# Gate values that travel with the rows, gathers that add, and a channel mix whose first norm runs inside the time mix

## The reference, cut to what matters

```python
x = x + delta_memory(layernorm(x))          # three recurrences, 16 chunks of work ("turns")
# mixture of experts: 8 experts, 2 of them per token
probs = softmax(xf @ w_router); topk_w, topk_idx = top_k(probs, 2)
h   = gelu(einsum('td,edh->teh', xf, w1) + b1)
out = (einsum('teh,ehd->ted', h, w2) + b2) * weights      # summed over the experts
x = x + out
# RWKV block on layernorm(x), here called x1
kvr = layernorm(x1, g1, b1) @ W_tm;  k, v, r = split(kvr), each mixed with x1 of the token before
y   = wkv(time_decay, time_first, k, v)                   # recurrence over tokens, log-sum-exp form
xa  = x1 + sigmoid(r) * y                                 # "time mix"
xp  = xa of the token before (the last token for token 0)
xn  = layernorm(xa, g2, b2)
kk  = (xn @ W_cm) * cmk + xp * (1 - cmk)
xc  = xa + sigmoid(xn * cmr + xp * (1 - cmr)) * (square(relu(kk)) @ W_cp)   # "channel mix"
x = x + xc
x = x + ffn(layernorm(x))                                 # gated, then two 1024x1024 layers, 256 out
```

## Time and profile before

| | |
|---|---|
| median of 3 runs | 2262.72 us (2259.93 to 2266.33) |
| profiled execution | 2248.27 us, of which its span 2246.4 us |
| PE busy | 1978.6 us, 88% of the span, 11554 matmuls |
| DVE busy | 1388.3 us, 62% |
| ACT busy | 930.4 us, 41% |
| POOL busy | 283.6 us, 13% |
| stages by start and end | delta memory 0 to 500, tail 500 to 564, experts 564 to 1008.5, time mix 1012 to 1317.7, handoff to 1344.9, channel mix to 1574.0, FFN to 2246.4 |

### The profile page before, as it was taken

One profiled execution on the slowest core, in us unless ns is written; L12 is line 12 of the kernel. 1 busy time (PEld: TensorE's weight loads), 2 busy tenths in 40 slices (PEclk: granted clock), 3 DMA queues, 4 the chain that ended last, 5 costly groups with the idle time before them and its releaser, 6 DMA issues. The chain is left out here.

```text
span 2246.4 us, 32147 instructions
## 1 busy us (share of the span) xinstructions
PE 1978.6 (88%) x11554; PEld 1695.3 (75%) x11554; DVE 1388.3 (62%) x2584; ACT 930.4 (41%) x1690; POOL 283.6 (13%) x241
## 2 busy tenths in 40 slices
PE   8999999995799999994664618998999999999999
PEld 5799998994799999993443406776788888888887
DVE  7557666665566766746999747887354453444442
ACT  4655555542223233225765636663322323323221
POOL 0010012244222222206332000000000000000000
PEclk9999999995899999997876859999999999999999
DMA  3399211113322222113121021341300000000000
GB/s 98 118 378 411 72 36 46 46 67 113 112 85 81 80 84 80 43 42 116 57 75 38 38 95 36 116 159 50 116 20 1 19 19 0 19 19 0 19 10 11
DMA packets 78626, 169.80 MB, mean 76 GB/s; under 512 B 7424, under 2 KB 41088, under 8 KB 78336
## 3 DMA queue, kind: packets, MB, share of 16 engines
q1 hardware_dynamic: 58624, 127.61, 15.8%
q0 software_dynamic: 9248, 30.42, 4.2%
q10 hardware_dynamic: 10640, 10.27, 1.4%
HBM read 95.66 MB, written 84.15 MB: 80 GB/s over the span
## 5 line engine op out<-in xcount | busy, mean ns | idle before, releaser
L1493 ACT ACTIVATE h<-bank,b1s 128x256 f32<-128x256 f32 x280 | 129.2, 475 | 297.1 <-PE bank L1347 241.8
L2464 ACT ACTIVATE gq<-bank,scl 128x512 f32<-128x512 f32 x128 | 88.3, 690 | 360.2 <-PE bank L2515 359.4
L2514 PE MATMUL bank<-hAh,ffn_h 128*128 128x512 f32 x512 | 202.7, 396 | 0.7 <-DVE gq L2392 0.7
L2514 PE MATMUL bank<-hBh,ffn_h 128*128 128x512 f32 x512 | 201.7, 394 | 0.0
L2515 PE MATMUL bank<-hAl,ffn_h 128*128 128x512 f32 x512 | 199.4, 389 | 0.0
L2515 PE MATMUL bank<-hBl,ffn_h 128*128 128x512 f32 x512 | 199.3, 389 | 0.0
L863 ACT ACTIVATE L<-bank 128x512 f32<-128x512 f32 x160 | 95.2, 596 | 152.0 <-PE bank L1118 151.3
L514 DVE TENSOR_TENSOR st<-st,bank 128x256 f32<-128x256 f32 x224 | 91.2, 419 | 105.7 <-PE bank L1125 104.4
L1118 PE MATMUL bank<-L 128*128 128x128 f32 x768 | 146.8, 280 | 0.0
L1125 PE MATMUL bank<-st,L 128*128 128x128 f32 x896 | 139.3, 282 | 4.7 <-DVE st L514 4.7
L1554 DVE TENSOR_TENSOR hsl<-h,hsh 128x512 fp32r<-128x512 f32 x140 | 136.4, 974 | 4.8
(11 more groups left out here) (419 smaller groups left out, 5543.8 us busy)
## 6 DMA issues: line engine op xcount, KB each, us to landing
z_by_expert<-zero SPq DMA_DIRECT2D x64, 512.0 KB, 14.9
st<-in_w_dram SPq DMA_DIRECT2D x16, 1024.0 KB, 6.5
ckb<-in_ffn_dram POOLq DMA_DIRECT2D x32, 352.0 KB, 3.5
moe_sorted<-yt ACTq DMA_DIRECT2D x37, 256.0 KB, 2.2
xg<-z_by_expert SPq DMA_DIRECT2D x36, 256.0 KB, 2.7
ffn_h<-ffn_copy SPq DMA_DIRECT2D x2, 4096.0 KB, 15.0
IN<-after_time_mix SPq DMA_DIRECT2D x15, 512.0 KB, 5.9
moe_sorted<-zero SPq DMA_DIRECT2D x8, 512.0 KB, 12.8
```

What stands on the lines that cost most here:

```text
L1493: nc.scalar.activation(h32[:, m, :], B[m % 4][:, 0:TT], ACT.Gelu_apprx_tanh, bias=b1s[:, e * KH + m:e * KH + m + 1]).then_inc(h_act, 1)
L2464: A_.activation(gq[:, m % 4, :], B[2 + m % 4][:, :], ACT.Gelu, scale=scl[:, off[nm] + m:off[nm] + m + 1]).then_inc(g_act, 1)
L2514: T.matmul(out, w, x[0], start=first, stop=False)
```

## The change

1. The row gets three more floats: the difference of the two gates, the second gate, and which expert is the first. Zero fills, scatters and the loads of `xg` move 259 floats a row instead of 256. `gates(b)` computes the values per block; the work at the end of the tail goes. Zero fills, then scatters, then loads keep their order.
2. The expert stage multiplies its result by the gate, so `moe_sorted` holds rows that only have to be added.
3. The gathers add into `x_tok` by themselves. POOL issues those of blocks 0 to 5 at once; DVE's eight multiply-adds a block are gone.
4. `x2T` is stored to `residual_sum` and POOL adds `YA` to it with an adding DMA (`add_to_sum`); `result(b)` waits for that of block b-1. Roots become exp(-0.5 ln).
5. The channel mix's weights are loaded by SP at the time mix's start and split by ACT (`high_weights`) and DVE (`low_weights`); `low_part(b+2)` moves to the end of iteration b; `keys_values` becomes `taken(b, 0)` and `taken(b, 1)`.
6. The channel mix goes through its blocks as 1 to 7, 0, and block 1's norm is done by the time mix's engines in their last two iterations (`first_...`); its buffers lie where `x_tok` was.

```diff
             def choose(b, n):
...
+                if n == 1:
+                    V.tensor_tensor(ge[:, GS], small[:, M2, blk(b)], small[:, M1, blk(b)], ALU.subtract).then_inc(ge_rdy, 1)
...
+            def gates(b):
+                dve.wait_ge(ge_d, b + 1)
+                go(V.tensor_reduce(ge[:, GD], three(ge[:, GA]), AX.X, ALU.add))
+                go(V.reciprocal(ge[:, GF], ge[:, GD]))
+                go(V.tensor_tensor(Z1[:, blk(b), GL], ge[:, GF], ge[:, GS], ALU.mult))
+                go(V.tensor_tensor(Z1[:, blk(b), DG], ge[:, GF], Z1[:, blk(b), GL], ALU.subtract))
...
+                at(u, 1, 7, gates)
                 at(u, 1, 7, take_ranks)
...
-            places(b5)
             out_scale(b7)
             residual(b7, 0)
             residual(b7, 1)
             stats(b7)
+            gates(b5)
+            places(b5)
...
+            def gate_exponentials(b):
+                act.wait_ge(ge_rdy, b + 1)
+                n = CPB * (NE + 1)
+                A_.activation(ge[:, 0:n], ge[:, 0:n], ACT.Exp).then_inc(ge_d, 1)
...
+                at(u, 0, 6, gate_exponentials)
...
+            def gate_of(e, t):
+                dve.wait_ge(rg_tk, t + 2)
+                V.scalar_tensor_tensor(sum_g[:, :], raw_g[:, :, WHO - D], float(e - 64), raw_g[:, :, DG - D], ALU.is_equal,
+                                       ALU.mult).then_inc(g_st, 1)
+                dve.wait_ge(g_st, t * 3 + 1)
+                V.tensor_tensor(own_g[:, 1, :], sum_g[:, :], raw_g[:, :, GL - D], ALU.add).then_inc(g_st, 1)
...
             def rows_split(n):
                 dve.wait_ge(xt_ps, n + 2)
+                V.tensor_copy(raw_g[:, :, :], xg[:, :, D:ZW]).then_inc(rg_tk, 1)
...
-                    V.tensor_tensor(yt[:, j, :], B[5 + j][:, 0:D], b2s[:, e, :], ALU.add).then_inc(y_rdy, 1)
+                    V.tensor_tensor(yt[:, j, :], B[5 + j][:, 0:D], b2s[:, e, :], ALU.add).then_inc(yb_rdy, 1)
...
+            def y_gated(n):
+                dve.wait_ge(yb_rdy, n * 2)
+                for j in range(2):
+                    V.tensor_scalar(yt[:, j, :], yt[:, j, :], own_g[:, 0, j:j + 1], None, ALU.mult).then_inc(y_rdy, 1)
+
+            def hand_on(t):
+                dve.wait_ge(y_rdy, t * 2 + 4)
+                V.tensor_copy(own_g[:, 0, :], own_g[:, 1, :]).then_inc(g_st, 1)
...
             def step(e, t, before, start):
+                gate_of(e, t)
                 rows_split(t + 1)
...
+                if not start:
+                    y_gated(t)
+                hand_on(t)
...
+            def gathers(b):
+                for n in range(2):
+                    for c in range(b * CPB, (b + 1) * CPB):
+                        if n == 1:
+                            pool.wait_ge(*landed(c, 0))
+                        elif c >= NG:
+                            pool.wait_ge(*landed(c - NG, 1))
+                        pool.indirect_dma_start(x_tok[:, c, :], None, ym_d, bass.IndirectOffsetOnAxis(sloty[:, c, n:n + 1].bitcast(u32), 0),
+                                                compute_op=ALU.add).then_inc(landed(c, n)[0], 16)
+
+            def add_to_sum(b):
+                pool.wait_ge(x2_out[b % 2], 16 * (b // 2 + 1))
+                pool.wait_ge(xa_rdy, b + 1)
+                pool.dma_start(byk(sx_d)[:, :, b * BT:(b + 1) * BT], tmp[:, 5, :, :], accum_op=ALU.add).then_inc(sx_out, 16)
+
+            for b in range(NB - 2):
+                gathers(b)
+            for b in range(NB):
+                add_to_sum(b)
+                if b < 2:
+                    gathers(NB - 2 + b)
...
                 if b >= 1:
-                    dve.wait_ge(xa_out, 32 * b)
+                    dve.wait_ge(xa_out, 16 * b)
+                    dve.wait_ge(sx_out, 16 * b)
...
+            def low_weights(n):
+                dve.wait_ge(cw_hi, n + 1)
+                w = (wcm, wcp)[n]
+                hi, lo = (a[:, :, :].rearrange("p k n -> p (k n)") for a in w)
+                V.tensor_tensor(lo, cst[n], f32(hi), ALU.subtract).then_inc(cw_rdy, 1)
...
+            def root_logs(b):
                 act.wait_ge(sq_rdy, SQ + b + 1)
                 cs = slice(b * CPB, (b + 1) * CPB)
-                A_.activation(small[:, VE1, cs], small[:, VE1, cs], ACT.Sqrt)
-                A_.activation(small[:, VE2, cs], small[:, VE2, cs], ACT.Sqrt).then_inc(sq_done, 1)
+                A_.activation(small[:, VE1:VE2 + 1, cs], small[:, VE1:VE2 + 1, cs], ACT.Ln).then_inc(lr_d, 1)
...
             for b in range(NB):
                 sums(b)
-                if b + 1 < NB:
-                    low_part(b + 1)
                 if b + 3 < NB:
                     variances(b + 3)
                 differences(b)
+                if b == NB - 2:
+                    first_centred()
+                if b == NB - 1:
+                    first_scaled()
...
                 values(b)
                 result(b)
+                if b + 2 < NB:
+                    low_part(b + 2)
+            first_low_part()
...
+            def place(b):
+
+                return (b + 1) % NB * BT
```

More of the change, by code:

```diff
@@ L12 @@
+import math
 import concourse.bass as bass
@@ L753, in _ @@
             choose(b6, 1)
+            gates(b6)
             take_ranks(b6)
@@ L758, in _ @@
             choose(b7, 1)
-            exponents_of_gates()
+            gates(b7)
             take_ranks(b7)
             places(b7)
[L763 to L766, removed]
             dve.wait_ge(rk_ps, NB + 1)
@@ L903, in rows @@
                 for c in range(b * CPB + 2 * h, b * CPB + 2 * h + 2):
-                    last = A_.activation(Z1[:, c, :], x_tok[:, c, :], ACT.Identity, bias=small[:, NM, c:c + 1],
+                    last = A_.activation(Z1[:, c, 0:D], x_tok[:, c, :], ACT.Identity, bias=small[:, NM, c:c + 1],
                                          scale=small[:, RST1, c:c + 1])
@@ L1009, in _ @@
                 columns(b6, k)
+            A_.activation(sc8[:, 5:6], sc8[:, 3:4], ACT.Sqrt)
             norm_root(b7)
@@ L1014, in _ @@
                 columns(b7, k)
-            act.wait_ge(sq_rdy, 8)
-            A_.activation(small[:, M2, :], small[:, M2, :], ACT.Exp)
-            A_.activation(LG[:, :, :], LG[:, :, :], ACT.Exp).then_inc(sq_done, 1)
+            gate_exponentials(b6)
+            gate_exponentials(b7)
         @block.tensor
@@ L1563, in _ @@
             expert_tiles(dve, step)
-            y(NE - 1, tile_count(dve))
+            total = tile_count(dve)
+            y(NE - 1, total)
+            y_gated(total)
         pblk.close()
@@ L1875, in columns, with taken @@
                 last.then_inc(xT_cp, 1)
-            def keys_values(b):
-                for i, o in ((0, 6), (1, 4)):
-                    act.wait_ge(km_ps, b * 3 + (i + 1))
-                    for k in range(KT):
-                        last = A_.activation(kvr[:, b % 2, i, k, :], B[o + k][:, :], ACT.Copy)
-                    last.then_inc(km_out, 1)
+            def taken(b, i):
+                act.wait_ge(km_ps, b * 3 + (i + 1))
+                for k in range(KT):
+                    last = A_.activation(kvr[:, b % 2, i, k, :], B[(6, 4)[i] + k][:, :], ACT.Copy)
+                last.then_inc(km_out, 1)
             def gates(b):
@@ L1982, in products, with first_mean, first_variance @@
                     last.then_inc(km_ps, 1)
+                    if b == NB - 1 and i == 0:
+                        first_mean()
+            def first_mean():
+                pe.wait_ge(avg_rdy, 1)
+                pe.wait_ge(cin_ld[0], 32)
+                for k in range(KT):
+                    last = T.matmul(B[2][:, :], avg[:, :], IN[:, 0, 0, k, :], start=(k == 0), stop=(k == KT - 1))
+                last.then_inc(mean_ps, 1)
+            def first_variance():
+                pe.wait_ge(sqr_rdy, 1)
+                for k in range(KT):
+                    last = T.matmul(B[3][:, :], avg[:, :], sq[:, k, :], start=(k == 0), stop=(k == KT - 1))
+                last.then_inc(var_ps, 1)
             normed(0)
@@ L2295, in down @@
                 last.then_inc(kh_rd, 1)
-            pe.wait_ge(avg_rdy, 1)
-            mean(0)
-            variance(0)
             for b in range(NB + 1):
```

274 lines of the change are left out of this document (155 added, 119 removed).

## The result

The median goes from 2265.82 us (20 runs) to 2260.67 (20 runs); the ratio is 0.9975, 95% interval 0.9966 to 0.9984. So the kernel is 5 to 6 us faster (4 to 8 by the interval), inside what I called no change, and the forecast was 2227 with 2256 as its upper end. One of the 20 executions after the change took 3333.88 us at a granted clock of 0.56; the ratio leaves it out.

A forecast was written before the change was run, and what follows sets the result against it. TensorE bounds experts and FFN, VectorE the time mix. Time mix -50.4, handoff -18.2, turns +1.5, tail +1.3, experts +0.7 and +29.4 sum to -35.7 from 2262.7: 2227 us, range 2197 to 2256.

The forecast's parts named there:

- The experts: Expert stage: gate operations held by GpSimd's subtractions make TensorE wait, six times 4.9 us (+29); the last tile adds 0.7.
- the scaling isn't held: Experts: GpSimd's subtractions hold the gate operations but not the 128x256 scaling; the forecast itself, 2227, chance 0.50.
- rival B: Experts: the scaling is held too; TensorE waits 7.4 plus 1.5 of clock, six times, +53 for +29: 2251, chance 0.20.
- The start of the time mix: Up to b0's result: low_part(0) starts at 1044.7 instead of 1041.1, then 54.2 us become about 48; net -2.7.
- the sums land no earlier: Start of the time mix: VectorE's 13.2 us of waits for gathers mostly stay.
- The tail: End of the turns: POOL's 5.8 us of idle time takes up places(b5), 7 us later; b6's slots come 1.2 later; +1.3.
- The turns: Delta memory: each block's gate_exponentials adds a table load to ACT, five blocks at 0.3: +1.5 us (0 to 5).
- Steady blocks: Time mix: VectorE loses 5.0 us of work a block, from 30.9 to 25.9, and sets the pace.
- the handoff: Time mix to channel mix: 27.2 us become 9.0, mostly the last adding DMA's landing, 7.4; -18.2 us.
- C: Experts: nothing is held, tiny operations slip between POOL's; 2198, chance 0.15.
- D: Time mix: the 512 KB adding DMA is slow; at 23 us the gain is gone, at 26 it is 2288; chance 0.06.
- E: Time mix: ACT's list, not DVE's, sets a block at 28 us: +15, 2242; chance 0.09.

The follow-up runs named there:

- run 2: Changed kernel, with TensorE's down product waiting for the bias addition that frees its bank, no longer for the gated rows: 2239.70 us, ratio 0.9905.
- run 3: Changed kernel, with the bias added in PSUM and the scaling reading PSUM, right behind it: 2231.02 us, ratio 0.9875.
- run 4: On run 3, all tiny gate operations of a tile placed behind the first pair's split: 2211.83 us, ratio 0.9782 to the kernel before.
- run 5: On G, the 64 gathers into x_tok made plain, replacing rows instead of adding: 2222.11 us, ratio 0.9830 to the kernel before.
- run 9: On run 5, gathers of blocks 3 to 5 issued only once x2T of blocks 0 to 2 is taken; other chip: 2190.14 us, ratio 0.9723.
- run 6: On G, the second channel weight split moved behind the first block's work: 2214.08 us, ratio 0.9779 to the kernel before.
- run 10: On G, variances(2) moved behind exponents(0), block 2's roots behind exps(0); second chip: 2198.64 us, ratio 0.9765 to the kernel before.
- G: The kernel of run 4: the changed kernel with the scaling reading PSUM and gate operations behind the first pair's split; 2211.83 us, ratio 0.9782.
- run 7: On G, no exponentials for blocks 0 to 4 in the turns, gates made of the differences themselves: 2211.58 us, ratio 0.9777.
- run 11: G with the tail's old order and the reorderings of run 6 and run 10; second chip: 2197.09 us, ratio 0.9763.
- run 12: Run 11 with the gathers of blocks 3 to 5 paced as in run 9; second chip: 2204.61 us, ratio 0.9789.

## Why the prediction was wrong, point by point

- **The experts, +30 forecast, +45 measured: the largest miss.** The step that failed is "the scaling isn't held", for which I took L374's 0.41 as proof of one port. In the profile after, twelve scalings of 128x256 were held, eleven for 4.6 to 4.7 us and one for 1.98. That was rival B, forecast at +53 with a wait of 7.4 six times; measured 6.9 and +45. Runs 2 to 4 take the cost away step by step (481.5, 475.1, 451.8 us for the stage). What I forecast for the gate operations is what run 3 shows alone: 3.3 us against 3.4, a copy of two columns held for 4.56, and +24 against +30. The 0.41 was also misread, and the trace of the kernel before could have told:

```profile
L435 DVE TENSOR_SCALAR small<-small x4: 165/174/175, 67.9 to 108.0; 128x16 f32<-128x16 f32 x4
L439 DVE TENSOR_SCALAR small<-small,beta x2: 226/228/229, 69.0 to 108.6; 128x16 f32<-128x16 f32 x2
L481 DVE TENSOR_SCALAR woN<-small_weights x1: 346/346/346, 23.4 to 23.4; 128x256 f32<-128x256 f32 x1
```

  L435 has no pointer, the other two have one each: a pointer adds some 0.05 us, and from 16 to 256 columns the time grows by 0.12, which is 0.5 ns a column, the pace of the casts that GpSimd holds (`hsh`, 512 columns in 0.427). By these figures my estimate for 256 columns and two pointers is 0.40, L374's time: it ran at the fast pace, not at half of it. The same scaling reading PSUM takes 0.47 to 0.49, against 0.35 from SBUF. The Trainium skill, "SBUF — State Buffer", Who interferes with whom, lists the tensor-scalar form among those that can take the port shared with GpSimd. The trace agrees, and I had let a misread duration overrule it.
- **The start of the time mix, -2.7 forecast, +9.6 measured.** The step that failed is "the sums land no earlier": they land later. I had costed the gathers at 1.26 each and asked of the add only whether it was late in bulk. GpSimd needs at least 1.55 to issue one, and 24 of them stand ahead of the first result; the row of 48, which I had done 60 us after the first gather, is done at 101. Runs 5 and 9 (81.3 with plain ones, where my working had 79.8), 6 (nothing) and 10 (2 us) put it there. The weight split was costed right and does not count: `low_part(0)`, which I had at 31.9 after the first gather, starts at 32.1 with plain gathers (run 9) and at 36.1 with adding ones.
- **The tail, +1.3 forecast, +4.6 measured.** The step that failed is that POOL's idle time of 5.8 us takes up the later `places(b5)` and the rest runs as before. The first half held: the scatters of b6 start 26.6 us after the end of the turns in G, against 25.1 and 25.5 before. But GpSimd then idles 3.6 us ahead of b7's scatters, because VectorE starts `take_logits(b7)` late. With G's order this wait is 4.1 us in the profile after and 4.8 to 10.3 in runs 2 to 7, where the tail takes 57.1 to 59.9; in runs 9 and 10, on the other chip, it is 2.4 and the tail 54.4 and 54.3, only 1.7 over the 52.4 and 52.9 of runs 11 and 12 with the old order. The old order has 1.4 to 2.5 everywhere. So my 1.3 fits where that wait does not grow, and what makes it grow stays open.
- **The turns, +1.5 forecast, nothing that shows** (run 7, with 0.3 us between the medians). The 2 to 11 us of the profiles are of the size by which two profiles of one kernel differ.
- **What held.** Steady blocks (174.7 forecast, 175.8 measured), block b3's stall gone, the handoff (9.0 against 7.4), the adding DMA of 512 KB hidden in the loop, the FFN untouched. Rivals C, D and E did not occur.
- **The sum.** -35.7 forecast; with the measured terms in place of mine it is 45.4 + 9.6 + 4.6 + 0 - 46.5 - 19.8 = -6.7, and the medians show -5.2. The same sum for G is 0.8 + 9.8 + 4.4 - 46.3 - 19.5 = -50.8, and its medians show -50.2: no large term is missing.

## What to carry to other kernels

Small work placed on VectorE beside GpSimd's passes over SBUF isn't small: what has both ends in SBUF can wait until GpSimd's pass ends, up to 5 us here, and everything queued behind it waits too. Give it an operand in PSUM and place the rest behind what TensorE needs next; the two gave 45 us of the expert stage here (496.4 to 451.8). And before a duration is taken as a pace, compare two widths: the fixed part, pointers with it, can be more than half of a short operation. A transfer that takes over an engine's work has an issue price on its own engine, and the first blocks, which nothing covers, pay it. And where two profiles of one kernel differ by more than the change does, profile the old kernel twice before explaining anything.

## What the runs showed of the hardware that I had not expected

- An adding gather of 128 rows takes GpSimd 1.55 us at the least (median 1.85) to issue and lands in 4.1; a plain one 0.95 and 2.8.
- A tensor-scalar operation of 128x256 from SBUF to SBUF takes 0.35 us with one pointer and 0.41 with two, and up to 4.69 beside a pass of GpSimd; the same reading PSUM takes 0.47 to 0.49, beside GpSimd's casts too.
- With 48 plain gathers issued 1.25 us apart, VectorE stood idle for 18.5 us and TensorE between single products, behind nothing that the profile names; with a pause in the row, and on another chip, it did not happen. The adding ones, 1.86 apart, did no such thing in the time mix.
- One kernel's profiles differ by up to 9 us in a stage of 300 us in which TensorE is almost always busy (286.6 of 303.0), and by 0.2 us in all of the time mix, where VectorE sets the time.
